# A graph network layer pair on one core: rows of x and of the result laid out by four successive nodes per partition

## The chip, the core and the metric

The kernel runs on one core of a Trainium2 chip. The metric is the device time of one execution in microseconds (us), 556.91 us as the median of three runs (556.08 to 558.59). Engines are named as in the profile: PE is TensorE's matmul, PEld its weight load, DVE VectorE, ACT ScalarE, POOL GpSimd; SPq and ACTq are the queues on which SyncE and ScalarE issue their transfers.

## The reference

There are N = 12500 nodes with rows of 128 numbers, and 200000 edges sorted by their destination `dst`, each with a row of 64 and one of 128 numbers. All is fp32. Two layers are applied, each as x + layer(relu(layernorm(x))):

```python
# layer 0, with h = relu(layernorm(x))
aggregated = segment_sum(edge_attr_64 @ W_edge.T, dst) / clip(degree, 1)
x = x + concat([h @ W_self.T, aggregated @ W_neigh.T], 1) @ W_final.T + b_final
# layer 1, with h = relu(layernorm(x))
agg = segment_sum(edge_attr_128, dst)
x = x + relu(concat([h, agg], 1) @ W1 + b1) @ W2 + b2
```

## The kernel before

**The sums of edges.** The edges are cut into 128 chunks of some 1600, taken one in each step t of the program. SyncE loads a chunk's two kinds of rows into one of five slots (`ring128`, `ring64`, L394), and waits for PE to be done with the chunk five steps earlier before it does. DVE builds one-hot matrices (L1013), PE multiplies edge rows by them (L631, L633 for the 128 features, L649 for the 64, L654 and L658 for the counts), and DVE adds the result to `agg` at a place read at run time (L1043). `agg` lies with features on partitions and nodes along the free dimension: 3 planes, the first with the 128 summed features, the other two with the 64 and the degree.

**The nodes.** They are taken in 25 groups: group 0 has 256 nodes, groups 1 to 23 have 512, group 24 the last 468. A group has 2 or 4 tiles of 128 nodes (`tiles_of`), and x lies in `x0[partition, tile, feature]`: node j*128 + p of a group is row p of tile j. `SEQ` is the order in which groups are finished, group 24 first and group 0 last. A table made before the program is built (`SELF`, `TAKE`) gives the step at which each group's work is put among the chunks: x is loaded six steps ahead of its use (`load_x`, L828 to L831), ACT normalizes it, PE transposes tile by tile (`turn`, L669) and multiplies by the weights (`own_part`, L678). Once all of a group's sums are complete, `neigh` (L694) takes 128 columns of `agg` as the stationary operand for each tile and each of planes 1 and 2, so that the product comes out with nodes on partitions. `hidden` multiplies with the weights `w1b` stationary and the group's 512 columns of plane 0 as the moving operand (L706), then with `w1a` and the transposed h (L708). `output` (L715) brings nodes back on partitions, DVE adds (L1157), and ACT issues the store (`store`, L839 to L842).

Of an fp32 product PE's records show two, each with a weight load and a matmul; a transpose has one. So the 98 tiles give 424 records on L694 (some groups have their sums in two places, which are then both multiplied), and 54 on L706.

**The tables.** In the first 46 us PE also transposes the table of destinations, `table` (L583). Its stationary operand is 32 partitions by 128 columns, read in steps of `R` elements: `.rearrange("c (p r) -> c r p", r=R)`. R is 13 for the first of its four calls, and 3, 6 and 4 for the three that follow.

Of the kernel before, what the change touches and what calls it, by code (L numbers as in the profile page):

```python
# [14 lines left out]
P = 128  # L15
# [12 lines left out]
GN = 4  # L28
# [7 lines left out]
X_SEMS = 8  # L36
# [39 lines left out]
def build_gnn(nc, x, dst, edge_attr_128, edge_attr_64, W_self, W_neigh, W_edge, W_final, b_final,  # L76
# [5 lines left out]
    NT = -(-N // P)  # L82
    LAST_N = N - (NT - 1) * P
# [19 lines left out]
    NG = 1 + -(-(N - FIRST_W) // GW)  # L103

    def begin_of(g):
        return FIRST_W + (g - 1) * GW if g else 0

    def end_of(g):
        return min(N, begin_of(g + 1))

    def tiles_of(g):
        return -(-(end_of(g) - begin_of(g)) // P)
# [87 lines left out]
    for q in range(NG - 1, -1, -1):  # L200
# [2 lines left out]
            t -= 1  # L203
        SELF.insert(0, t)
    assert SELF[0] >= 0, SELF
    TICKS = CH + 13

    def x_done(q):

        return sum(32 if SEQ[k] == NG - 1 else 16 for k in range(q % X_SEMS, q + 1, X_SEMS))  # L210


    HOT_SUMS, ADDED, LOADED, in_slot = [0], [0], [], [0] * SLOTS
# [37 lines left out]
    with ExitStack() as ctx:  # L251
# [128 lines left out]
        @block.sync  # L380
        def _(sp):
            sp.wait_ge(s_dst_clear, 1)
            z0 = 32 * UNITS * P
            sp.dma_start(dst_i[0:32, :], dst[0:z0].rearrange("(r e) -> r e", r=32)).then_inc(s_dst0, 16)

            def load_edges(t):
                c = ORDER[t]
                slot, e0, R = t % SLOTS, first_edge(c), run_of(c)
                if t >= SLOTS:
                    sp.wait_ge(s_mm, t - SLOTS + 1)  # L390
                nb = 2 if c == CH - 1 else PARTS[c // 32]
                e1 = e0 + nb * R * P
                for ring, feats in ((ring128, edge_attr_128), (ring64, edge_attr_64)):
                    sp.dma_start(ring[:, slot, 0:nb * R, :].rearrange("p (b r) f -> p b (r f)", b=nb),  # L394
                                 feats[e0:e1, :].rearrange("(b p r) f -> p b (r f)", p=P, r=R)).then_inc(s_load[slot], 16)
                    if c == CH - 1:
                        sp.dma_start(ring[0:H, slot, 6, :], feats[e1:E, :]).then_inc(s_load[slot], 16)

            load_edges(0)
            for r0, r1, e0, w in ((96, 126, first_edge(96), 12 * P), (126, 127, first_edge(126), 12 * P),  # L400
                                  (127, 128, first_edge(127), LAST_E), (32, 96, z0, 12 * P)):
                sp.dma_start(dst_i[r0:r1, 0:w], dst[e0:e0 + (r1 - r0) * w].rearrange("(r e) -> r e", e=w)).then_inc(s_dst, 16)
            rest = 12 * P - LAST_E
            sp.dma_start(dst_i[127:128, LAST_E:12 * P], dst[E - rest:E].rearrange("(r e) -> r e", r=1)).then_inc(s_dst, 16)
            for t in range(1, CH):
                load_edges(t)
            sp.wait_ge(s_store, 16 * (NG + 1))

            def general():
                sp.dma_start(gen_dst_i, dst.rearrange("(p e) -> p e", p=GP)).then_inc(s_gdst, 16)  # L410

                def group(g):
                    with sp.Fori(0, PASSES) as w:
                        with sp.Fori(0, GC) as c:
                            sp.wait_ge(s_gmm, (g * PASSES + w) * GC + c + 1)
                            for ring, feats in ((gen_r128, edge_attr_128), (gen_r64, edge_attr_64)):
                                sp.dma_start(ring, feats.rearrange("(p c r) f -> p c (r f)", p=GP, r=GR)[
                                    :, bass.ds(c, 1), :].rearrange("p o f -> p (o f)")).then_inc(s_gload, 16)
                    sp.wait_ge(s_gst, g * 32 + 32)
                    if not isinstance(g, int):  # L420
                        rows = x[bass.ds(g * GW, GW), :].rearrange("(j p) f -> p j f", p=P)
                        sp.dma_start(x0[:, 0:2, :], rows[:, 0:2, :]).then_inc(s_gx, 16)
                        sp.dma_start(x0[:, 2:4, :], rows[:, 2:4, :]).then_inc(s_gx, 16)
                        sp.wait_ge(s_gstep, g * GSTEPS + GSTEPS + 1)
                        rows = out[bass.ds(g * GW, GW), :].rearrange("(j p) f -> p j f", p=P)
                        sp.dma_start(rows[:, 0:2, :], x0[:, 0:2, :]).then_inc(s_gst, 16)
                        sp.dma_start(rows[:, 2:4, :], x0[:, 2:4, :]).then_inc(s_gst, 16)
                    else:
                        n0 = g * GW
                        sp.dma_start(x0[:, 0, :], x[n0:n0 + P, :]).then_inc(s_gx, 16)  # L430
                        sp.dma_start(x0[0:LAST_N, 1, :], x[n0 + P:N, :]).then_inc(s_gx, 16)
                        sp.wait_ge(s_gstep, g * GSTEPS + GSTEPS + 1)
                        sp.dma_start(out[n0:n0 + P, :], x0[:, 0, :]).then_inc(s_gst, 16)
                        sp.dma_start(out[n0 + P:N, :], x0[0:LAST_N, 1, :]).then_inc(s_gst, 16)
                        sp.wait_ge(s_gst, g * 32 + 64)

                every_group(sp, group)

            otherwise(sp, general)
# [3 lines left out]
        def _(pool):  # L443
# [19 lines left out]
            const(nc.gpsimd.memset(w_c[H:H + 1, 1, D:D + 1], 1.0))  # L463
            assert own_const[0] == N_CONST

            nc.gpsimd.memset(x0[:, NT - 1, :], 0.0).then_inc(s_xpad, 1)

            def steps_of(k):

# [102 lines left out]
        def _(pe):  # L572
# [108 lines left out]
            def neigh(q):  # L681
                g = SEQ[q]
                pe.wait_ge(s_added, ADDED[min(CH, TAKE[q])])
                for i, (k, _) in enumerate(FOLDS):
                    if k == q:
                        pe.wait_ge(s_fold, 2 * i + 2)
                if q:
                    pe.wait_ge(s_x1, q)
                else:
                    pe.wait_ge(s_untab, 4)  # L690
                parts = [(a, k) for a in columns_of(g) for k in range(2)]
                for j in range(tiles_of(g)):
                    for i, (a, k) in enumerate(parts):
                        last = nc.tensor.matmul(ps_nb[:, j // 2, j % 2, :], agg[:, 1 + k, a + j * P:a + (j + 1) * P], w_c[:, k, :],  # L694
                                                start=i == 0, stop=i == len(parts) - 1)
                last.then_inc(s_nb, 1)

            def hidden(q):
                g = SEQ[q]
                w = tiles_of(g) * P  # L700
                if q:
                    pe.wait_ge(s_hr, q)
                else:
                    pe.wait_ge(s_gen, 1)
                for i, a in enumerate(columns_of(g)):
                    nc.tensor.matmul(ps_hid[:, 0:w], w1b[:], agg[:, 0, a:a + w], start=i == 0, stop=False)  # L706
                pe.wait_ge(s_tpc, tp_use["n", q] + 1)
                nc.tensor.matmul(ps_hid[:, 0:w], w1a[:], h2T[:, 0:w], start=False, stop=True).then_inc(s_hid, 1)  # L708

# [100 lines left out]
        def _(act):  # L810
# [6 lines left out]
            def load_x(q):  # L817
                g = SEQ[q]
                n0, n1, j0 = begin_of(g), end_of(g), tile_of(g)
                if q >= X_SEMS:  # L820
                    act.wait_ge(s_x[q % X_SEMS], x_done(q - X_SEMS))
                if SCRATCH[0] <= g <= SCRATCH[1]:
                    act.wait_ge(s_viol, 1)
                    act.wait_ge(s_wsb, 3)
                if g == NG - 1:
                    act.wait_ge(s_xpad, 1)
                    m = n1 - LAST_N
                    act.dma_start(x0[:, j0:NT - 1, :], x[n0:m, :].rearrange("(j p) f -> p j f", p=P)).then_inc(s_x[q % X_SEMS], 16)  # L828
                    act.dma_start(x0[0:LAST_N, NT - 1, :], x[m:n1, :]).then_inc(s_x[q % X_SEMS], 16)
                else:  # L830
                    act.dma_start(x0[:, j0:j0 + tiles_of(g), :], x[n0:n1, :].rearrange("(j p) f -> p j f", p=P)).then_inc(s_x[q % X_SEMS], 16)  # L831

            def store(q):
                g = SEQ[q]
                n0, n1, j0 = begin_of(g), end_of(g), tile_of(g)
                act.wait_ge(s_rowc, row_use["n", q] + 1)
                if g == NG - 1:
                    m = n1 - LAST_N
                    act.dma_start(out[n0:m, :].rearrange("(j p) f -> p j f", p=P), x0[:, j0:NT - 1, :]).then_inc(s_store, 16)  # L839
                    act.dma_start(out[m:n1, :], x0[0:LAST_N, NT - 1, :]).then_inc(s_store, 16)  # L840
                else:
                    act.dma_start(out[n0:n1, :].rearrange("(j p) f -> p j f", p=P), x0[:, j0:j0 + tiles_of(g), :]).then_inc(s_store, 16)  # L842

            def inputs(t):
                for q in range(NG):
# [480 lines left out]
```

## Time and profile before

| | |
|---|---|
| median of three runs | 556.91 us |
| the profiled execution's own time | 556.97 us |
| its span, first to last instruction | 555.1 us |
| PE busy, share of the span | 503.9 us, 91% |
| DVE / POOL / ACT busy | 390.6 / 368.4 / 151.5 us |
| granted TensorE clock, mean | 0.966 |
| bytes moved | 169.53 MB, mean 305 GB/s |

"Busy" is the time in which at least one of an engine's instructions runs. PE records overlap (a 64-column matmul is shown as 228 ns long, yet a new one starts every 28 ns on average), so the cost of a matmul in a stream is read from the chain of work, where each piece is the time until the next one begins. Idle time of PE put down to "issue" is time in which it waited for nothing that the profile shows. The DMA share is the mean busy share of the core's 16 DMA engines.

### The profile page before, as it was taken

How to read it: one execution, taken by the hardware profiler on the slowest of the kernel's cores; microseconds unless marked ns; L12 is line 12 of the kernel's file. 1: busy time of each engine (PE TensorE's matmuls, PEld its weight loads, DVE VectorE, ACT ScalarE, POOL GpSimd, SP SyncE). 2: the span in 40 equal slices, each digit the busy share in tenths (PEclk: the TensorE clock that was granted, in tenths of full speed). 3: DMA queues.
4: the chain of work that ended last, by engine and by line, in shares of the span. 5: the costliest groups of instructions: out<-in, count | busy, mean ns of one | idle time of the engine just before them, and what ended most of it. 6: DMA issues, size and time to landing. Idle time of an engine off the chain costs nothing.

```text
span 555.1 us, 25952 instructions
## 1 busy us (share of the span) xinstructions
PE 503.9 (91%) x10989; PEld 450.1 (81%) x10989; DVE 390.6 (70%) x1230; ACT 151.5 (27%) x353; POOL 368.4 (66%) x524
## 2 busy tenths in 40 slices
PE   5568879899989999999999999998999999999993
PEld 4457768789878898888988898888888888988782
DVE  5434698776896768967798688789669877567322
ACT  0011101332233332342234224333323332313101
POOL 2735947667577776785768777885866765845730
PEclk9767899999999999999999999999999999999996
DMA  8924999999999998999999999999999998959910
GB/s 282 388 58 148 380 354 359 374 339 322 312 347 303 341 349 303 367 301 313 341 323 355 333 331 323 369 320 304 325 320 358 329 322 277 382 221 310 378 41 13
DMA packets 113229, 169.53 MB, mean 305 GB/s; under 512 B 5486, under 2 KB 84310, under 8 KB 113111
## 3 DMA queue, kind: packets, MB, share of 16 engines
q1 hardware_dynamic: 85843, 154.42, 79.7%
q10 hardware_dynamic: 27268, 13.43, 8.3%
q8 instruction: 88, 1.44, 1.1%
q14 instruction: 30, 0.25, 0.1%
HBM read 161.43 MB, written 6.40 MB: 302 GB/s over the span
## 4 chain that ended last, share of the span: by engine, by line
PE 81%; issue 6%; DVE 4%; DVEq 1%; ACT 0%; POOL 0%
PE ps L631 28%; PE ps L649 15%; PE ps L694 9%; PE ps L706 5%; PE ps L633 5%; PE ps L678 5%; PE ps L669 4%; PE ps L715 4%; PE ps L708 4%; DVE agg L1043 2%; PE ps L658 1%; DVE x L1157 1%; DVE onehot L1013 1%; DVE bn L1137 0%; DVEq L1043 0%
## 5 line engine op out<-in xcount | busy, mean ns | idle before, releaser
L631 PEld LDWEIGHTS ps<-onehot,ring 128*64 128x64 f32 x3126 | 198.8, 141 | 30.8 <-issue 22.6
L631 PE MATMUL ps<-onehot,ring 128*64 128x64 f32 x3126 | 217.2, 228 | 6.5 <-issue 4.6
L633 PE MATMUL ps<-onehot,ring 128*64 128x64 f32 x3126 | 217.3, 228 | 4.7 <-issue 4.7
L522 POOL TENSOR_TENSOR hot_part<-onehot 128x384 bf16<-128x384 f32 (+2 forms) x128 | 116.7, 912 | 152.3 <-DVE onehot L1013 150.6
L633 PEld LDWEIGHTS ps<-onehot,ring 128*64 128x64 f32 x3126 | 198.8, 141 | 5.4 <-issue 5.4
L1043 DVE TENSOR_TENSOR agg<-ps,agg 128x128 f32 (+1 forms) x319 | 95.0, 298 | 120.1 <-PE ps L658 95.9
L1013 DVE TENSOR_TENSOR onehot<-iota_win,rel 128x384 f32<-128x384 f32 (+3 forms) x192 | 164.5, 857 | 0.2
L649 PE MATMUL ps<-onehot,ring 128*64 128x64 f32 x3126 | 121.9, 226 | 7.2 <-issue 7.1
L649 PEld LDWEIGHTS ps<-onehot,ring 128*64 128x64 f32 x3126 | 109.2, 141 | 7.4 <-issue 7.2
L694 PEld LDWEIGHTS ps<-w_c,agg 128*128 128x128 f32 x424 | 49.8, 191 | 7.3 <-DVE agg L1043 3.7
L694 PE MATMUL ps<-w_c,agg 128*128 128x129 f32 x424 | 52.3, 276 | 3.3 <-issue 2.3
L522 POOL TENSOR_TENSOR hot_sum<-hot_part 128x128 bf16<-128x128 bf16 x96 | 44.7, 466 | 7.5
L875 ACT ACTIVATE hn<-x,nmr,rstd 128x128 f32<-128x128 f32 x98 | 40.4, 483 | 22.5 <-DVE nmr L1104 22.4
L903 ACT ACTIVATE h<-x,nmr,rstd 128x128 f32<-128x128 f32 x98 | 40.4, 484 | 15.5 <-DVE nmr L1149 15.5
L918 ACT ACTIVATE hid<-ps,b_col 128x512 f32<-128x512 f32 (+1 forms) x25 | 17.0, 679 | 93.2 <-PE ps L708 93.2
L500 POOL TENSOR_TENSOR x<-x,b_bc 128x512 f32<-128x512 f32 (+1 forms) x25 | 35.6, 1424 | 10.2 <-ACT h L903 10.2
L522 POOL TENSOR_TENSOR hot_sum<-hot_sum,hot_part 128x128 bf16<-128x128 bf16 x64 | 34.9, 545 | 5.0
L508 POOL MEMSET agg<- 128x1536 f32 (+2 forms) x26 | 35.5, 1366 | 0.0
L487 POOL TENSOR_TENSOR x<-x,b_bc 128x512 f32<-128x512 f32 (+1 forms) x25 | 34.2, 1369 | 0.0
L883 ACT COPY hT<-ps 128x512 f32<-128x512 f32 (+1 forms) x25 | 14.5, 579 | 70.5 <-PE ps L669 70.5
L890 ACT COPY own<-ps 128x512 f32<-128x512 f32 (+1 forms) x25 | 14.5, 579 | 67.3 <-PE ps L678 64.4
L494 POOL TENSOR_TENSOR x<-x,own 128x512 f32<-128x512 f32 (+1 forms) x25 | 31.9, 1275 | 0.0
(118 smaller groups left out, 568.7 us busy)
## 6 DMA issues: line engine op xcount, KB each, us to landing
ring<-in_edge_attr_dram SPq DMA_DIRECT2D x95, 768.0 KB, 5.5
ring<-in_edge_attr_dram SPq DMA_DIRECT2D x96, 384.0 KB, 7.0
ring<-in_edge_attr_dram SPq DMA_DIRECT2D x32, 832.0 KB, 6.2
ring<-in_edge_attr_dram SPq DMA_DIRECT2D x32, 416.0 KB, 7.7
x<-in_x_dram ACTq DMA_DIRECT2D x23, 256.0 KB, 6.3
out_dram<-x ACTq DMA_DIRECT2D x23, 256.0 KB
x<-in_dst_dram SPq DMA_DIRECT2D x1, 384.0 KB
x<-in_dst_dram SPq DMA_DIRECT2D x1, 208.0 KB, 3.6
```

Of the source, the lines that this page charges most:

```text
L487: nc.gpsimd.tensor_tensor(rows, rows, b0_bc[:, :].unsqueeze(1).to_broadcast([P, nt, D]), ALU.add).then_inc(s_xb, 1)
L500: nc.gpsimd.tensor_tensor(rows, rows, b2_bc[:, :].unsqueeze(1).to_broadcast([P, nt, D]), ALU.add).then_inc(s_x1b, 1)
L508: nc.gpsimd.memset(agg[:, :, a:b], 0.0).then_inc(s_zero, 1)
L522: nc.gpsimd.tensor_tensor(out, a, b, ALU.add).then_inc(s_hotsum, 1)
L631: nc.tensor.matmul(bank[0:H, o:o + WIN], ring128[0:K, slot, u, 0:H], hots, start=u == 0, stop=r == R - 1, skip_group_check=True)
L633: nc.tensor.matmul(bank[H:P, o:o + WIN], ring128[0:K, slot, u, H:D], hots, start=u == 0, stop=r == R - 1, skip_group_check=True)
L649: nc.tensor.matmul(bank[feats, o:o + WIN], ring64[0:K, slot, u, :], onehot[0:K, hot, u, :], start=False, stop=True, skip_group_check=True)
L694: last = nc.tensor.matmul(ps_nb[:, j // 2, j % 2, :], agg[:, 1 + k, a + j * P:a + (j + 1) * P], w_c[:, k, :], start=i == 0, stop=i == len( ...
L875: last = nc.scalar.activation(hn[:, j, :], x0[:, j0 + j, :], ACT.Relu, bias=nmr1[:, u, j:j + 1], scale=rstd1[:, u, j:j + 1])
L903: last = nc.scalar.activation(h2[:, j, :], x0[:, j0 + j, :], ACT.Relu, bias=nmr2[:, u, j:j + 1], scale=rstd2[:, u, j:j + 1])
L1013: made = nc.vector.tensor_tensor(onehot[:, t % HOTS, a:b, :], iota_win[:, :].unsqueeze(1).to_broadcast([P, b - a, WIN]), rel[:, c // 32, a ...
L1043: nc.vector.tensor_tensor(here, ps[:, t % BANKS, o:o + w * WIN].rearrange("p (a n) -> p a n", a=w), here, ALU.add).then_inc(s_added, 1)
```

## The change

Row p of tile j in a group with `nt` tiles now holds node p*nt + j instead of node j*128 + p. A partition so has four successive nodes (two in group 0), which are 2048 successive bytes (1024) in x and in the result: one transfer row instead of four of 512 bytes. The last group's 468 nodes fill 117 partitions of all four of its tiles, where before they filled three tiles and 84 partitions of the fourth; so one transfer loads and one stores it instead of two, and the area cleared before its load has four tiles instead of one.

`agg` keeps its order. So PE picks every fourth column of it (every second in group 0): as stationary operand for `neigh`, 128 columns in steps of 4 elements (16 bytes), and as moving operand for `hidden`, 512 columns in the order 0, 4, 8, ..., 1, 5, ....

```diff
@@ the end of SyncE's program
-            sp.wait_ge(s_store, 16 * (NG + 1))
+            sp.wait_ge(s_store, 16 * NG)
@@ GpSimd, before its first sums
-            nc.gpsimd.memset(x0[:, NT - 1, :], 0.0).then_inc(s_xpad, 1)
+            nc.gpsimd.memset(x0[:, NT - GN:NT, :], 0.0).then_inc(s_xpad, 1)
@@ TensorE, neigh(q)
-                        last = nc.tensor.matmul(ps_nb[:, j // 2, j % 2, :], agg[:, 1 + k, a + j * P:a + (j + 1) * P], w_c[:, k, :],
+                        last = nc.tensor.matmul(ps_nb[:, j // 2, j % 2, :], agg[:, 1 + k, a + j:a + tiles_of(g) * P:tiles_of(g)], w_c[:, k, :],
                                                 start=i == 0, stop=i == len(parts) - 1)
@@ TensorE, hidden(q)
-                    nc.tensor.matmul(ps_hid[:, 0:w], w1b[:], agg[:, 0, a:a + w], start=i == 0, stop=False)
+                    sums_128 = agg[:, 0, a:a + w].rearrange("f (p j) -> f j p", j=tiles_of(g))
+                    nc.tensor.matmul(ps_hid[:, 0:w], w1b[:], sums_128, start=i == 0, stop=False)
@@ ScalarE, load_x(q)
-                    m = n1 - LAST_N
-                    act.dma_start(x0[:, j0:NT - 1, :], x[n0:m, :].rearrange("(j p) f -> p j f", p=P)).then_inc(s_x[q % X_SEMS], 16)
-                    act.dma_start(x0[0:LAST_N, NT - 1, :], x[m:n1, :]).then_inc(s_x[q % X_SEMS], 16)
-                else:
-                    act.dma_start(x0[:, j0:j0 + tiles_of(g), :], x[n0:n1, :].rearrange("(j p) f -> p j f", p=P)).then_inc(s_x[q % X_SEMS], 16)
+                nt, m = tiles_of(g), (n1 - n0) // tiles_of(g)
+                act.dma_start(x0[0:m, j0:j0 + nt, :], x[n0:n1, :].rearrange("(p j) f -> p j f", j=nt)).then_inc(s_x[q % X_SEMS], 16)
@@ ScalarE, store(q)
-                    act.dma_start(out[n0:n1, :].rearrange("(j p) f -> p j f", p=P), x0[:, j0:j0 + tiles_of(g), :]).then_inc(s_store, 16)
+                nt, m = tiles_of(g), (n1 - n0) // tiles_of(g)
+                act.dma_start(out[n0:n1, :].rearrange("(p j) f -> p j f", j=nt), x0[0:m, j0:j0 + nt, :]).then_inc(s_store, 16)
```

The order of work on PE, DVE, POOL and SyncE is the same in both. On ACT two transfers fewer are issued. This is the head of ACT's program before, where the weights' transfers and then those of group 24's x stand:

```order
L815 DMA b_bc<-in_L_gnn_b_dram 128x128
L815 DMA b_col<-in_L_gnn_b_dram 128x1
L828 DMA x<-in_x_dram 128x3x128
L829 DMA x<-in_x_dram 84x128
L856 ACT_TABLE_LOAD
L856 COPY x<-ps 128x256
```

and this is the same place now:

```order
L818 DMA b_bc<-in_L_gnn_b_dram 128x128
L818 DMA b_col<-in_L_gnn_b_dram 128x1
L831 DMA x<-in_x_dram 117x512
L852 ACT_TABLE_LOAD
L852 COPY x<-ps 128x256
```

The shape of a full group's load goes from `128x4x128` to `128x512`, a row of 512 numbers in one piece; the store's goes the same way.

## Rows read from the trace of the kernel before

**Rows 1.** The page, sections 1 and 4 (busy; the chain that ended last).
```profile
PE 503.9 (91%) x10989; PEld 450.1 (81%) x10989; DVE 390.6 (70%) x1230; ACT 151.5 (27%) x353; POOL 368.4 (66%) x524
...
PE 81%; issue 6%; DVE 4%; DVEq 1%; ACT 0%; POOL 0%
```

**Rows 2.** Three stretches: length, PE busy (records), granted clock, DMA share, GB/s.
```profile
0.00:75.00 75.00, 49.07 (x930) 0.82 0.74 260
75.00:545.00 470.00, 451.17 (x10051) 1.00 0.93 319
545.00:555.10 10.10, 3.62 (x10) 0.51 0.06 18
```

**Rows 3.** Whom PE waited for, 75 to 545 us: total us, times, longest.
```profile
PE ps L649 <- issue: 5.2, 8, 1.4
PE ps L631 <- issue: 3.9, 3, 1.7
PE ps L633 <- issue: 2.7, 4, 1.0
PE ps L694 <- issue: 2.3, 2, 1.4
PE ps L694 <- DVE agg L1043: 1.1, 3, 0.6
PE ps L678 <- DVE x L1157: 1.0, 2, 0.7
PE ps L678 <- issue: 0.7, 1, 0.7
```

**Rows 4.** Whom SyncE's queue waited for, 75 to 555 us.
```profile
SPq L394 <- PE ps L658: 334.9, 113, 6.5
SPq L367 <- DMA out_dram<-x: 29.7, 1, 29.7
```

**Rows 5.** Page, sections 3 and 6: queues' packets, MB, share; issues, median us to landing.
```profile
q1 hardware_dynamic: 85843, 154.42, 79.7%
q10 hardware_dynamic: 27268, 13.43, 8.3%
...
ring<-in_edge_attr_dram SPq DMA_DIRECT2D x96, 384.0 KB, 7.0
...
x<-in_x_dram ACTq DMA_DIRECT2D x23, 256.0 KB, 6.3
```

**Rows 6.** The chain, 300 to 318 us: start us, us until the next piece, what.
```profile
301.77 1.05 PE ps L706 x2
302.83 0.86 PE ps L708 x2
...
307.49 1.79 PE ps L694 x16
```

**Rows 7.** Groups of PE's instructions by shape: busy us, mean ns of one.
```profile
L694 PE MATMUL ps<-w_c,agg 128*128 128x129 f32 x424 | 52.3, 276 | 3.3 <-issue 2.3 <-DVE agg L1043 1.1
...
L706 PE MATMUL ps<-agg,w1b 128*128 128x512 f32 x52 | 28.3, 633 | 0.0
```

**Rows 8.** Timeline, PEld, the tables' loads in steps of 3, 6 and 4 elements.
```profile
23.53 1.45 PEld L583 LDWEIGHTS ps<-ident,x 32*128 32x128 f32 x12 [6.99 <-DVE x L993]
...
33.66 1.68 PEld L583 LDWEIGHTS ps<-ident,x 32*128 32x128 f32 x12 [4.17 <-DVE x L993]
...
44.21 1.51 PEld L583 LDWEIGHTS ps<-ident,x 32*128 32x128 f32 x12 [3.93 <-DVE x L993]
```

**Rows 9.** Lines 583 and 600, their loads: ns min/median/max; then L583's three stretches.
```profile
L583 PEld LDWEIGHTS ps<-ident,x x49: 188/208/236, 7.4 to 45.5; 32*128 32x128 f32 x49
...
L600 PEld LDWEIGHTS ps<-ident,x x2: 183/204/224, 35.4 to 35.5; 128*128 128x128 f32 x2
...
44.20:45.90 1.70, 1.64 (x12) 1.51 (x12) 0.50 0.57 229
```

**Rows 10.** Timeline, the start: POOL's clear, ACT's first loads of x, DVE's wait.
```profile
2.63 0.31 POOL L461 MEMSET w_c<- 128x258 f32 x1
...
3.29 0.21 POOL L466 MEMSET x<- 128x128 f32 x1
...
5.84 0.50 ACTq L828 DMA_DIRECT2D x<-in_x_dram  x1
...
10.91 0.99 POOL L522 TENSOR_TENSOR hot_part<-onehot 128x384 bf16<-128x384 f32 x1 [7.41 <-DVE onehot L1013]
11.93 0.16 DVE L1167 CAST firsts<-x 32x2 f32<-32x2 int32 x1 [1.11 <-DMA x<-in_dst_dram]
```

More of the change, by code:

```diff
@@ L205, in build_gnn @@
     assert SELF[0] >= 0, SELF
+    assert all((end_of(g) - begin_of(g)) % tiles_of(g) == 0 for g in range(NG))
     TICKS = CH + 13
     def x_done(q):
-        return sum(32 if SEQ[k] == NG - 1 else 16 for k in range(q % X_SEMS, q + 1, X_SEMS))
+        return sum(16 for k in range(q % X_SEMS, q + 1, X_SEMS))
     HOT_SUMS, ADDED, LOADED, in_slot = [0], [0], [], [0] * SLOTS
@@ L836, in store @@
                 act.wait_ge(s_rowc, row_use["n", q] + 1)
[L837 to L841, printed above, removed]
-                    act.dma_start(out[n0:n1, :].rearrange("(j p) f -> p j f", p=P), x0[:, j0:j0 + tiles_of(g), :]).then_inc(s_store, 16)
+                nt, m = tiles_of(g), (n1 - n0) // tiles_of(g)
+                act.dma_start(out[n0:n1, :].rearrange("(p j) f -> p j f", j=nt), x0[0:m, j0:j0 + nt, :]).then_inc(s_store, 16)
             def inputs(t):
```

## The prediction

> **What bounds the kernel now.** I read the busy times and the chain of work that ended last first. PE is busy 91% of the span, and 81% of the chain is PE's own work, with 6% "issue" and 4% DVE [rows 1]. Then the stretches: from 75 to 545 us PE is busy for 451.17 of 470 us at the full granted clock, so 18.8 us are left idle there; 75 us of start and 10 us of tail lie around it [rows 2]. Nearly all of that idle time is "issue" (5.2 + 3.9 + 2.7 + 2.3 + 0.7 = 14.8 us), none is a wait for a DMA of edges or of x [rows 3]. The reader is to see two things that look alike and are not: the DMA engines are as busy as PE (share 0.93), but it is SyncE that waits for PE, 113 times for 334.9 us together, before it may refill a slot [rows 4]. A load of edges lands some 7.0 us after its issue [rows 5], and with five slots it is issued four steps before its use; a step is 4.2 us (470 us over the 113 waits). The DMA side has some 9 us in hand at each step. PE sets the pace, so what counts is whether PE's new access patterns cost time; what the DMA saves is mostly hidden.
>
> **Term 1, the loads of L694 in steps of four.** Sixteen of its records take 1.79 us of the chain, 112 ns each [rows 6]. In that time 129 columns are streamed and the next 128 are loaded, so `agg` is read at 128/112 = 1.14 elements a ns. There are 424 records [rows 7]; the last 8 belong to group 0, with steps of two. All stand on the path, 424 x 0.112 = 47 us. What would steps of four do? No row shows this instruction with steps, but the tables' transposes load 128 fp32 columns in steps of 3, 6 and 4. Twelve such loads take 1.45, 1.68 and 1.51 us [rows 8]; take away the last one's length (some 0.21 us) and divide by eleven: 113, 134 and 118 ns from one load to the next. One load by itself is 208 ns in the median (188 to 236), and the same kind of load without steps, L600, is 183 and 224, mean 204, at a granted clock of 0.50 in both [rows 9]. So steps cost these loads nothing that can be seen, and at step four the chip reads 128/118 = 1.08 elements a ns or more. That is within 5% of what L694 needs. Bounds: 0 if the 118 ns is the transposes' own pace, and (118 - 112) x 424 = +2.5 us if it is the reading's limit; a gain is excluded, since a stepped read cannot fetch fewer bytes. I take 0, as the three step sizes show no trend (6 is slower than 4, but 3 equals the others).
>
> **Term 2, the moving columns of L706 in steps of four.** L708, which streams 512 contiguous columns twice, takes 0.86 us of the chain, 430 ns a record or 1.19 elements a ns; L706 takes 1.05 us, the same and a weight load that nothing hides [rows 6]. There are 52 such records on 512 columns [rows 7] and two of 256 in the tail. No row shows a moving fp32 operand with steps. The nearest is again the stepped load, 1.08 elements a ns at least. Bounds: 0 above, and 430 x (1.19/1.08 - 1) = 44 ns a record, x 54 = +2.4 us, below; again no gain. I take 0, because the rate that the stream needs is the rate at which the loads were seen to run, at one access per 16 bytes, with no sign of a limit.
>
> The Trainium skill speaks against this change: "SBUF — State Buffer", at its note on SBUF cachelines, says that SBUF reads in lines of 16 bytes, that full bandwidth wants two or more hits in a line, and that an access which crosses to a new line pays a penalty. A step of four fp32 elements meets every line once. By that rule terms 1 and 2 would not be 0; the page gives no price. Steps of 4 and of 6 elements in the tables' loads do the same, and [rows 9] show no penalty there, so by the trace the rule does not bind at this rate. What it would do if it did is the first rival.
>
> **Term 3, the transfers.** The queue of x and the result (ACT's, with the weights) takes 27268 packets for 13.43 MB and 8.3% of the engines' time; SyncE's takes 79.7% for 154.42 MB [rows 5]. Per packet that is 27 ns for 492 bytes against 82 ns for 1799, so 18.2 against 21.8 bytes a ns. With rows of 2048 bytes, ACT's queue at SyncE's rate would take 13.43/154.42 x 79.7 = 6.9%: 1.4 points less. A small packet is thus only a sixth dearer per byte. On the path this is worth nothing by itself: PE waits for no edges, x lands in 6.3 us with six steps, 25 us, of lead, and the slots' 9 us in hand is the cover. If that cover were gone, the price of 1.4 points would be 7.8 us of the span. One thing may profit: the "issue" waits. If they are fetches of PE's instructions that queue among data on the same engines (I have no row that proves it), they would shrink with the queueing. Bounds: 0, and, for a queue whose delay goes as load/(1 - load), 0.93 to 0.916 is 13.3 to 10.9, -18% of 14.8 us = -2.7 us. It could also be that larger packets hold a fetch up longer; the packets of 2048 bytes are no larger than the mean of those already there, so I bound that at +0.3 us. I take -0.4.
>
> **Term 4, the start and the end.** POOL's clear grows from 128 to 512 columns: 0.21 us now; from 128x258 at 0.31 us I get some 0.5. It ends near 3.9 us, ahead of ACT's load of x at 5.84, and POOL then waits for DVE until 10.91 [rows 10]: hidden. Without that cover it would be 0.3 us. ACT issues one transfer less there (0.5 us); next on ACT is a copy that waits long for PE. Group 24's x now goes in larger packets beside the first edges and destinations, for whose last part DVE waits 1.11 us at 11.93; its 234 KB are there either way, so -0.1 to +0.3 us, taken as 0. At the end, group 0's 128 KB are 128 packets instead of 256 after the last DVE instruction; at 27 ns and 16 engines the whole is 0.43 us now, so at most -0.1 us. I take 0 for both together.
>
> **Sum.** 0 + 0 - 0.4 + 0 on the profiled execution's own 556.97 us (span 555.1 and 1.9 around it) is 556.6 us. That execution stands 0.06 us above the median of the three runs, so no correction: 556.6 us.
>
> **Rivals.**
>
> *Steps halve the reading rate of the moving operand (slower).* Place: L706, each group's hidden layer. Then each record of 512 columns takes another 430 ns, on PE, with nothing to hide it: 52 x 0.43 = +22.4 us, 579 us. If the stationary reads halved as well, a load of 128 would need some 0.11 us more, 416 x 0.107 = +44.5 us on top, 623 us. It decides from the point where a stepped read falls under 1.14 elements a ns. For it: moving and stationary operands need not be fetched alike, and only loads with steps were seen, on 32 partitions and at half the clock. Against it: those loads, at the same absolute rate. This is the cacheline rule of the Trainium skill turned into a mechanism.
>
> *Steps cost a tenth (slower).* The upper bounds of terms 1, 2 and 4 come true: +2.5 + 2.4 + 0.3 = +5.2, 562 us. For it: 118 against 112 ns. Against it: a transpose has a tail of its own in those 118 ns.
>
> *The instruction waits shrink (faster).* Term 3 at its low end with a shorter end: 554.1 us, and less if I mistake how they depend on the load; 553 at the least. For it: they are 14.8 us of PE's idle time, and DMA is 93% busy in the same stretch. Against it: only 1.4 points of load go.
>
> *The transfers stay in rows of 512 bytes.* Then term 3 is 0 and the time 557.0. The shapes of the changed kernel's transfers, 128x512, speak against it; it makes no difference to the chances.
>
> **How the numbers follow.** No change: 0.67. The instruction waits shrink by enough: 0.13. A tenth: 0.08. Halved, in one of its forms: 0.12. A measurement of this kernel can tell about 0.5% (2.8 us) from no change; its own three runs span 0.45%. The range goes from 553.0 (the low ends of terms 3 and 4 and the scatter of the median, 1 us) to 562.8 (the tenth's 562 with 0.6 of scatter); outside are the halved case and some 0.03 below. Faster by over 0.5%: 0.13 and a little of the likeliest case, 0.14. Slower: 0.08 + 0.12, 0.20 less 0.01 where the tenth stays under the bound, 0.19. Same: 0.67.
>
> **What would show it.** Right: sixteen records of L694 still take 1.79 us of the chain and two of L706 1.05 us; ACT's queue falls from 27268 packets to some 8500 (25000 rows of 512 bytes become 6282 packets) and to about 7%; SyncE still waits for PE over 110 times; PE's "issue" waits stay between 12 and 17 us. Wrong: L706 at 1.9 us for its two records or L694 over 1.9 us for sixteen; a wait of PE for edges after 75 us; the "issue" total under 10 us with the span shorter by as much, which would say that I priced the DMA's load too low.

## The result, and the profile after

The changed kernel takes 619.42 us (median of four runs, 617.27 to 620.37) against 557.75 us for the kernel before on the same chip: ratio 1.111, 95% interval 1.106 to 1.116. The forecast of 556.6 us was wrong, and so was its range. The time is near the 623 us of the first rival, halved reading of both operands, to which the forecast gave 0.12 in all its forms.

Sections 1, 3 and 4 of the page (busy; the queue of x and the result with packets, MB and share; the chain) now read:

```profile
PE 571.9 (93%) x10989; PEld 497.5 (81%) x10989; DVE 387.5 (63%) x1230; ACT 151.3 (25%) x353; POOL 366.9 (59%) x524
...
q10 hardware_dynamic: 8612, 13.43, 6.1%
...
PE 85%; DVE 4%; issue 3%; DVEq 1%; ACT 0%
```

PE has 68 us more to do with the same 10989 records [rows 1]. The queue of x and the result fell from 27268 packets to 8612, as the prediction said [rows 5]. The chain, 306 to 313 us and at the end (start us, us until the next piece, what; lines 696, 709 and 711 are 694, 706 and 708 of before), says where the 68 us are:

```profile
306.59 1.98 PE ps L709 x2
308.56 0.86 PE ps L711 x2
309.42 3.61 PE ps L696 x16
...
603.76 1.22 PE ps L696 x8
...
609.19 0.85 PE ps L709 x2
```

Sixteen records of `neigh` take 3.61 us instead of 1.79, and two of `hidden` 1.98 instead of 1.05; L711, contiguous, is as before at 0.86 [rows 6]. Group 0, last, reads in steps of two: its eight records take 1.22 us (1.17 before), its two of `hidden` 0.85 as before (these at a granted clock of 0.50 in both kernels, so they say nothing of the full clock). The groups by shape (busy us, mean ns of one) say the same:

```profile
L696 PE MATMUL ps<-w_c,agg 128*128 128x129 f32 x424 | 102.1, 396 | 3.3 <-DVE agg L1039 1.7 <-issue 1.4
L709 PE MATMUL ps<-agg,w1b 128*128 128x512 f32 x52 | 52.3, 1103 | 0.0
```

Then the stretches (length, PE busy with its records, clock, DMA share, GB/s), the middle one from the same work of the start to group 0's `neigh`. First the kernel after, then that before cut at the same work:

```profile
0.00:73.10 73.10, 45.97 (x936) 0.86 0.76 269
73.10:603.70 530.60, 521.10 (x10037) 0.99 0.81 282
603.70:616.70 13.00, 4.83 (x18) 0.66 0.04 14
```

```profile
75.00:541.90 466.90, 450.01 (x10043) 1.00 0.94 321
```

The bill: 26 x (3.61 - 1.79) = 47.3 us for `neigh` and 26 x (1.98 - 1.05) = 24.2 us for `hidden`, 71.5 us together; PE's busy time in the middle stretch grew by 71.1. Its idle time there shrank from 16.9 to 9.5 us, 7.4 us given back, and the stretch grew by 63.7. Start and tail are 1.9 and 0.2 us shorter: 61.6 us, the difference of the spans (616.7 - 555.1). The two stepped reads so account for PE's added work to within 0.4 us. PE's "issue" waits there are 7.7 us together, 14.8 before [rows 3]. SyncE still waits for PE 112 times, 393.6 us now against 334.9 [rows 4]: the transfers have more in hand than before, not less.

### The profile page after: what moved, and what is told of

Same layout as the page of the kernel before. It is cut to its first block, busy times and chain, and to the rows that moved or that the text cites. A ratio compares the mean times of both kernels' runs of the same rounds, so it can differ in the third digit from the quotient of the medians.

```text
span 616.7 us, 25950 instructions
## 1 busy us (share of the span) xinstructions
PE 571.9 (93%) x10989; PEld 497.5 (81%) x10989; DVE 387.5 (63%) x1230; ACT 151.3 (25%) x353; POOL 366.9 (59%) x524
## 3 DMA queue, kind: packets, MB, share of 16 engines
q10 hardware_dynamic: 8612, 13.43, 6.1%
## 4 chain that ended last, share of the span: by engine, by line
PE 85%; DVE 4%; issue 3%; DVEq 1%; ACT 0%
PE ps L633 25%; PE ps L696 16%; PE ps L651 14%; PE ps L709 8%; PE ps L718 4%; PE ps L671 4%; PE ps L680 4%; PE ps L635 4%; PE ps L711 3%; DVE agg L1039 1%; PE ps L660 1%; DVE onehot L1009 0%; DVEq L1017 0%; DVE x L989 0%; DVEq L1039 0%
## 5 line engine op out<-in xcount | busy, mean ns | idle before, releaser
L633 PEld LDWEIGHTS ps<-onehot,ring 128*64 128x64 f32 x3126 | 197.7, 141 | 33.4 <-issue 27.3
L633 PE MATMUL ps<-onehot,ring 128*64 128x64 f32 x3126 | 215.6, 227 | 8.9 <-issue 7.0
L635 PE MATMUL ps<-onehot,ring 128*64 128x64 f32 x3126 | 215.7, 227 | 1.8 <-issue 1.8
L635 PEld LDWEIGHTS ps<-onehot,ring 128*64 128x64 f32 x3126 | 197.7, 141 | 1.9 <-issue 1.9
L1009 DVE TENSOR_TENSOR onehot<-iota_win,rel 128x384 f32<-128x384 f32 (+3 forms) x192 | 157.5, 821 | 0.2
L651 PE MATMUL ps<-onehot,ring 128*64 128x64 f32 x3126 | 118.2, 223 | 2.9 <-issue 2.9
L651 PEld LDWEIGHTS ps<-onehot,ring 128*64 128x64 f32 x3126 | 106.2, 139 | 3.0 <-issue 2.7
L696 PEld LDWEIGHTS ps<-w_c,agg 128*128 128x128 f32 x424 | 100.5, 326 | 6.5 <-DVE agg L1039 4.4
L696 PE MATMUL ps<-w_c,agg 128*128 128x129 f32 x424 | 102.1, 396 | 3.3 <-DVE agg L1039 1.7
L709 PE MATMUL ps<-agg,w1b 128*128 128x512 f32 (+1 forms) x54 | 53.4, 1085 | 0.0
L1116 DVE TENSOR_SCALAR deg<-ps 128x4 f32<-128x4 f32 (+1 forms) x25 | 4.0, 161 | 70.2 <-PE ps L696 70.2
L502 POOL TENSOR_TENSOR x<-x,b_bc 128x512 f32<-128x512 f32 (+1 forms) x25 | 35.7, 1427 | 10.3 <-ACT h L899 10.3
L711 PEld LDWEIGHTS ps<-h2T,w1a 128*128 128x128 f32 x50 | 10.5, 213 | 33.1 <-issue 32.8
```

Source lines behind the costliest of these rows:

```text
L502: nc.gpsimd.tensor_tensor(rows, rows, b2_bc[:, :].unsqueeze(1).to_broadcast([P, nt, D]), ALU.add).then_inc(s_x1b, 1)
L633: nc.tensor.matmul(bank[0:H, o:o + WIN], ring128[0:K, slot, u, 0:H], hots, start=u == 0, stop=r == R - 1, skip_group_check=True)
L635: nc.tensor.matmul(bank[H:P, o:o + WIN], ring128[0:K, slot, u, H:D], hots, start=u == 0, stop=r == R - 1, skip_group_check=True)
L651: nc.tensor.matmul(bank[feats, o:o + WIN], ring64[0:K, slot, u, :], onehot[0:K, hot, u, :], start=False, stop=True, skip_group_check=True)
L709: nc.tensor.matmul(ps_hid[:, 0:w], w1b[:], sums_128, start=i == 0, stop=False)
L1009: made = nc.vector.tensor_tensor(onehot[:, t % HOTS, a:b, :], iota_win[:, :].unsqueeze(1).to_broadcast([P, b - a, WIN]), rel[:, c // 32, a ...
```

## The experiments

**One part at a time.** The first three kernels split the change. The kernel before, run beside them, took 557.35 us (median of 23 runs); gains and losses in us are the ratio's, on that time. The diffs of this section show only the operands that change. `e1_loads` is the kernel before with this:

```diff
-agg[:, 1 + k, a + j * P:a + (j + 1) * P]
+agg[:, 1 + k, a + j:a + tiles_of(g) * P:tiles_of(g)]
```

> The kernel before, with one part of the change: neigh takes its stationary columns of agg in steps of four; x and the result keep their old rows, so each node's neighbour part is that of another node. Theory A (a step of 16 bytes halves the rate at which a product's fp32 operand is read, stationary and moving alike): sixteen records of L694 go from 1.79 to 3.61 us of the chain, 416 x 0.114 = +47 us, less some 7 us of instruction waits that get shorter: 598 us (592 to 605), ratio 1.07. Rival B (the loads are free, as the tables' stepped loads were, and the changed kernel's time came from elsewhere, such as the new rows of x): 557 us. Rival C (the slowing needs the new transfers as well): 557 to 570 us.

Measured: 599.31 us, ratio 1.0767 (1.071 to 1.082), +42.7 us. `e2_moving` is the kernel before with the other read:

```diff
-nc.tensor.matmul(ps_hid[:, 0:w], w1b[:], agg[:, 0, a:a + w], start=i == 0, stop=False)
+sums_128 = agg[:, 0, a:a + w].rearrange("f (p j) -> f j p", j=tiles_of(g))
+nc.tensor.matmul(ps_hid[:, 0:w], w1b[:], sums_128, start=i == 0, stop=False)
```

> The kernel before, with one part of the change: hidden streams its moving columns of agg in the order 0, 4, 8, ..., 1, 5, ...; the rest is as before, so each node's summed edges are those of another node. Theory A: two records of L706 go from 1.05 to 1.98 us of the chain, 26 x 0.93 = +24 us, less a few us of shorter instruction waits: 578 us (572 to 582), ratio 1.04. Rival B (moving operands are free): 557 us.

Measured: 576.02 us, ratio 1.0334 (1.028 to 1.039), +18.6 us. In each chain only the stepped line is slower; that of `e1_loads`, then that of `e2_moving`:

```profile
299.52 1.06 PE ps L706 x2
300.58 0.86 PE ps L708 x2
301.44 3.61 PE ps L694 x16
```

```profile
290.80 1.97 PE ps L707 x2
292.77 0.86 PE ps L709 x2
293.63 1.78 PE ps L694 x16
```

Each read costs by itself what it costs in the changed kernel, without the new transfers. `e3_rows` is the changed kernel with both edits undone, so it has the transfers alone.

> The changed kernel's transfers (rows of 2048 bytes, the last group in one transfer) with the old contiguous reads of agg by TensorE, so sums and nodes don't match. It prices the gain that the change was to bring. Theory A (PE sets the pace, edges have 9 us in hand): within 1.5 us of 557. Rival (PE's instruction waits are fetches that queue among data on the DMA engines): down to 554. Rival (larger packets hold the fetches up): up to 560.

Measured: 555.14 us, ratio 0.9956 (0.992 to 0.9992), -2.5 us (0.4 to 4.5): a gain that is barely told from none. Its q10 has 6.6% of the engines' time:

```profile
q10 hardware_dynamic: 8612, 13.43, 6.6%
```

The three add up to 42.7 + 18.6 - 2.5 = 58.8 us, against 61.9 measured for the whole (0.111 x 557.75); the intervals of the four cover the difference.

**What a step costs, alone.** `m1_full` and `m2_half` have streams of like instructions on an idle chip, such as

```python
for _ in range(12):
    last = nc.tensor.matmul(ps[:, 0, 0:128], wide[0:128, 0:512:4], wide[0:128, 0:128], start=True, stop=True)
```

> Nothing of the layers is computed; the result is zeros. TensorE alone runs streams of like instructions at the full clock on an idle chip (no other engine, no transfers): fp32 products with the 128 stationary columns in steps of 1, 2, 3, 4, 6, 8, 13; with 512 moving columns in steps of 1, 2, 3, 4, 6, 8; with 32 rows; transposes of 128 and of 32 rows; bf16 loads and moving columns. Theory A1 (a read needs two hits in a 16-byte line): steps 1 and 2 alike, some 110 ns a record, from step 4 on twice as long whatever the step, step 3 in between; transposes too, if they are at the full clock. Theory A2 (only products of fp32 in two records suffer): transposes at all steps alike at 110 to 120 ns. Theory A3 (128 rows at once are needed for it): 32 rows alike at all steps. Rival (contention with DVE, POOL or transfers on the same memory made it): no step costs anything here.

> The same streams, shorter, each after a pause of TensorE long enough that the granted clock is half; the result is zeros. Theory A4 (the limit is one of the memory in absolute time, about 1.77 ns for each new line): at half clock contiguous products take 213 ns a record and steps of four next to nothing more; transposes, which read 128 columns in 107 ns at half clock, would take 226. Theory A5 (the limit is in TensorE's own clocks): a step of four doubles the record here too, to some 430 ns. The tables' transposes in the kernel (118 ns at step four and half clock) should be met again by the streams of 32 rows.

The timeline of PE in `m1_full` (start us, us, line, shape, records); lines 51, 54, 57, 60, 69 are products with their 128 loaded columns in steps of 1, 2, 3, 4 and 13, lines 81, 84, 87, 93 have 512 moving columns in steps of 2, 3, 4 and 8, lines 105 and 108 are transposes of 128 rows with loads in steps of 4 and 13, lines 111, 114 and 120 transposes of 32 rows with loads in steps of 1, 2 and 4:

```profile
31.17 2.84 PE L51 MATMUL ps<-wide 128*128 128x128 f32 x24
33.84 2.99 PE L54 MATMUL ps<-wide 128*128 128x128 f32 x24
36.67 4.33 PE L57 MATMUL ps<-wide 128*128 128x128 f32 x24
40.84 5.76 PE L60 MATMUL ps<-wide 128*128 128x128 f32 x24
...
57.52 6.32 PE L69 MATMUL ps<-wide 128*128 128x128 f32 x24
...
79.07 4.66 PE L81 MATMUL ps<-wide 128*128 128x512 f32 x10
83.57 6.92 PE L84 MATMUL ps<-wide 128*128 128x512 f32 x10
90.32 9.17 PE L87 MATMUL ps<-wide 128*128 128x512 f32 x10
...
108.25 9.36 PE L93 MATMUL ps<-wide 128*128 128x512 f32 x10
...
122.95 2.08 PE L105 MATMUL ps<-ident,wide 128*128 128x128 f32 x16
124.87 2.00 PE L108 MATMUL ps<-ident,wide 128*128 128x128 f32 x16
126.80 1.67 PE L111 MATMUL ps<-ident,wide 32*128 32x32 f32 x24
128.31 3.04 PE L114 MATMUL ps<-ident,wide 32*128 32x32 f32 x24
...
133.91 3.06 PE L120 MATMUL ps<-ident,wide 32*128 32x32 f32 x24
```

With the last one's length taken off, the pace of a product's load is 112, 118, 174, 233 and 257 ns. Moving columns go at 450, 675, 899 and 918 ns a record. So a step of two is nearly free, three costs half as much again, four doubles it, and from there on it hardly grows. Neither transfers nor other engines are needed for it. The transposes are another matter. With 128 rows a step of four takes (124.87 - 122.95)/16 = 120 ns at the full clock, where a product takes 233. With 32 rows it is 63 ns with contiguous columns, and 120 ns with a step of two, both at the full clock, as the granted clock in the stretches shows (the number behind the count of records); by line 120 TensorE had fallen to half, and a step of four took the same 120 ns:

```profile
126.80:128.30 1.50, 1.50 (x25) 1.00 0.00 0
128.30:131.00 2.70, 2.70 (x26) 1.00 0.00 0
...
133.90:136.70 2.80, 2.80 (x26) 0.50 0.03 6
```

A load in steps of four goes at about 0.9 ns a column in a transpose and at 1.8 ns in a product. With a step of two the two operations are alike, 120 and 118 ns.

At half clock, the loads of eight product records in steps of 1 and of 4, and of twelve transposes of 32 rows in steps of 1 and of 4 (timeline of PEld in `m2_half`); then, from PE's timeline, eight product records on 32 rows in steps of 1 and of 4:

```profile
29.82 1.78 PEld L194 LDWEIGHTS ps<-wide 128*128 128x128 f32 x8 [29.82 <-issue]
...
62.16 1.94 PEld L206 LDWEIGHTS ps<-wide 128*128 128x128 f32 x8 [9.02 <-POOLq L50]
...
246.14 1.35 PEld L274 LDWEIGHTS ps<-ident,wide 32*128 32x128 f32 x12 [9.23 <-POOLq L118]
278.55 1.51 PEld L286 LDWEIGHTS ps<-ident,wide 32*128 32x128 f32 x12 [9.37 <-POOLq L130]
```

```profile
105.37 2.07 PE L222 MATMUL ps<-wide 32*128 32x128 f32 x8 [8.38 <-POOLq L66]
116.17 2.23 PE L226 MATMUL ps<-wide 32*128 32x128 f32 x8 [8.73 <-POOLq L70]
```

This run's profile prints a clock of 1.00 throughout, but the contiguous stream goes at (1.78 - 0.33)/7 = 207 ns, about half the pace of line 51: TensorE was at its lower level. (In `m1_full`, contiguous moving columns go at 855/512 = 1.67 ns each in line 78, 73.4 to 77.2 us, where the granted clock is 0.52; 207/128 is 1.62.) There, a step of four costs a product 230 ns and a transpose 118 (the 1.51 us of [rows 8] to the digit). The 230 is what a step of four costs at the full clock too. So the limit is a time, not a count of TensorE's clocks, and A4 is right for products; it is wrong for transposes, which it put at 226. On 32 rows a step of four adds 0.16 us to eight product records, as on 128 (1.94 - 1.78), so the number of rows plays no part and A3 is wrong, as far as the half clock shows: in `m1_full` too the stepped stream on 32 rows (line 75, 235 ns) ran at a granted clock of 0.52, and no run has one at the full clock.

**Lines or steps.** `m3_pairs` has only moving patterns that tell the two apart, as

```python
wide[:, 0:2048].rearrange("k (c r) -> k c r", r=8)[:, :, 3:5]
```

> Nothing of the layers is computed; the result is zeros. TensorE alone at the full clock, fp32 products of 512 moving columns: contiguous; pairs of neighbours inside one 16-byte line with steps of 8 between pairs (0 1, 8 9, and 1 2, 9 10); pairs that straddle two lines (3 4, 11 12); fours in one line; steps of 4; the changed kernel's order (0 4 8 ..., then 1 5 9 ...); one column 512 times. Theory of lines (what costs is each change of 16-byte line, some 1.75 ns, against 0.83 ns that a column takes in the array): contiguous and fours 430 ns a record, pairs inside a line 450, straddling pairs and steps of four 900, one column 430. Rival theory of steps (each column whose address isn't the next costs extra): both kinds of pairs alike, between 450 and 900, and one column 512 times slow. bf16, one record, steps of 2, 4 and 8 elements: by lines 220, 450 and 900 ns.

Its timeline: line 51 is contiguous, 54 has pairs 0 1, 57 pairs 1 2, 60 the straddling pairs 3 4, 63 fours, 66 steps of four, 87 the changed kernel's order, 90 one column 512 times.

```profile
32.56 4.46 PE L51 MATMUL ps<-wide 128*128 128x512 f32 x10
36.85 4.75 PE L54 MATMUL ps<-wide 128*128 128x512 f32 x10
41.44 4.75 PE L57 MATMUL ps<-wide 128*128 128x512 f32 x10
46.02 9.16 PE L60 MATMUL ps<-wide 128*128 128x512 f32 x10
55.00 4.47 PE L63 MATMUL ps<-wide 128*128 128x512 f32 x10
59.31 9.16 PE L66 MATMUL ps<-wide 128*128 128x512 f32 x10
...
92.28 9.35 PE L87 MATMUL ps<-wide 128*128 128x512 f32 x10
101.45 4.49 PE L90 MATMUL ps<-wide 128*128 128x512 f32 x10
```

Per record: 430, 459, 459, 898, 431, 898, about 900 and 433 ns. Pairs cost about the same as steps of two while both lie in one 16-byte line and double when they straddle two. The theory of steps is wrong, that of lines holds: in a product, each change of line costs 898/512 = 1.75 ns, against 430/512 = 0.84 ns that a column takes in the array at the full clock. Lines of 8 bytes would have split the pairs 1 2, and lines of 32 would have held 3 4 together. This run tells the theories apart for moving columns only; for loads the steps of two and three fit lines (118 ns for 64 changes of line, 174 for 96, so 1.84 and 1.81 ns each).

**Two kernels that keep part of the change.** Both compute the whole layer pair. `e4_pairs` has two successive nodes per partition in each pair of tiles (`hidden`'s moving columns and the stores, not shown, follow the same order):

```diff
-agg[:, 1 + k, a + j * P:a + (j + 1) * P]
+agg[:, 1 + k, a + j // 2 * 2 * P + j % 2:a + (j // 2 + 1) * 2 * P:2]
-x[n0:n1, :].rearrange("(j p) f -> p j f", p=P)
+x[n0:n1, :].rearrange("(b p j) f -> p b (j f)", p=P, j=2)
```

> The whole layer pair with two successive nodes per partition instead of four: rows of 1024 bytes in x and the result, agg read in steps of two fp32 elements (8 bytes), two reads in each 16 bytes. Theory A with a limit at one read per 16-byte line (group 0, in steps of two, cost the changed kernel 1.22 us for eight loads against 1.17): PE as before, 557 us within 1.5, and less by what the rows bring. Rival (any step costs in proportion, or the two-level order of columns does): 590 us or more.

Measured: 558.22 us, ratio 1.0035 (1.0002 to 1.0069).

```profile
300.81 1.10 PE ps L707 x2
...
306.56 1.89 PE ps L694 x16
```

Steps of two are not quite free: 26 x 0.10 + 26 x 0.05 = +3.9 us on PE, and +2.0 measured (0.1 to 3.8). That leaves some 2 us for the rows of 1024 bytes, in line with `e3_rows`, but no more than the scatter of the runs. `e5_act` has rows of 2048 bytes and gives the reordering to ScalarE. This is one of its three places, against the changed kernel; the copy of the transposed h and the reading of `hidden`'s result are reordered too:

```diff
+nc.scalar.copy(apart_t[:, i, :, 0:w].rearrange("f k (j p) -> f k j p", p=P),
+               agg[:, 1:3, at:at + w].rearrange("f k (p j) -> f k j p", j=nt))   # at the head of step TAKE[q]
-agg[:, 1 + k, a + j:a + tiles_of(g) * P:tiles_of(g)]
+apart_t[:, columns_of(g).index(a), k, j * P:(j + 1) * P]
```

> The whole layer pair with four nodes per partition and rows of 2048 bytes, TensorE reading contiguous columns only: ScalarE (27% busy) copies planes 1 and 2 of a group's sums into tile order ahead of neigh, writes the transposed h in node order, and reads the hidden layer's result from PSUM in steps of four; hidden reads agg contiguously in node order. Theory A (TensorE's stepped reads were the whole loss; rows alone are worth -2.4 us): 555 us (553 to 557) if the copies, some 1.2 us for each of 41 places, are done before neigh is reached in its step. Rival (the copy comes late, or ScalarE's stepped access is slow as well, so that neigh waits 1 us or more in each of 25 groups): 565 to 590 us.

Measured: 591.66 us, ratio 1.0552 (1.049 to 1.061); there are 27 copies, not the 41 that the expectation counted. PE's lines are near their old times (`neigh`'s records 299 ns in the mean, 276 before and 396 in the changed kernel), and it waits instead. First `neigh`'s group; then whom PE waited for (total us, times, longest); then whom ACT waited for:

```profile
L699 PE MATMUL ps<-w_c,apart_t 128*128 128x129 f32 x424 | 59.1, 299 | 20.2 <-ACT apart_t L921 20.2
```

```profile
PE ps L699 <- ACT apart_t L921: 20.2, 15, 3.0
...
PE ps L720 <- ACT own L888: 4.1, 2, 2.6
...
PE ps L673 <- ACT hT L881: 3.1, 1, 3.1
```

```profile
ACT apart_t L921 <- DVE agg L1059: 100.5, 20, 9.9
```

A copy takes 2.0 us, and it stands at the head of ACT's step, where it waits for DVE's last addition with all of ACT's other work behind it. The rival was right in both its forms. The copy comes late, and ScalarE's stepped access is slow as well: its copy of the transposed h, now written in steps of four, takes 1.11 us instead of 0.58. PE's three waits are 27 us, and `neigh`'s records are busy for 6.8 us more than before (59.1 against 52.3 [rows 7]); the loss is 31 us. The profiled execution was 4 us above the median, and how the loss splits was not pursued. With some 2.5 us to win, neither kernel that computes the whole layer pair beat the kernel before.

## Why the prediction was wrong

**What bounds the kernel** was right: PE set the pace before and after, and of the 71.1 us that PE gained in work in the middle stretch all but 7.4 lengthened it. The cover on the DMA side stood.

**Term 1** is the step that failed. It priced `neigh`'s stepped loads by the tables' stepped loads, "at the same absolute rate", and took 0 with a bound of +2.5 us; it cost 47.3 us. The rate of [rows 8, 9] was real, and `m2_half` meets it again, but it belongs to transposes. A stepped read in a product is limited at 1.75 to 1.8 ns a line, in a transpose at 0.9 ns a column. The bound was one of another operation, put forward as if it were one of the memory. The rows were misread too: 113, 118 and 134 ns for steps of 3, 4 and 6 rise with the step, where the prediction saw no trend. `m2_half` shows no rise over more steps (118, 111, 118, 136 and 112 ns for 2, 3, 4, 6 and 13), so this misreading is not what made the term fail. The comparison also hid the sign of a limit: at half clock L583 and the contiguous L600 look alike because a contiguous load takes TensorE 103 ns there anyway (line 274 of `m2_half`, (1.35 - 0.22)/11), against 118 at a step of four; `m1_full` shows 63 against 120 ns at the full clock.

**Term 2** failed in the same way: 0 taken, +2.4 us as the bound, 24.2 us measured, where the moving operand meets the same limit per line. The prediction noted that "moving and stationary operands need not be fetched alike"; in a product they meet the same limit at a step of four (899/512 = 1.76 and 233/128 = 1.82 ns a column). What wasn't alike was product and transpose.

**The rule that was set aside** was right for products. The Trainium skill's "SBUF — State Buffer", note on SBUF cachelines, wants two or more hits in a 16-byte line; the trace agrees, with 459 ns for pairs in a line and 898 for pairs across two. Where the note names four fp32 elements as the stride that is free, the measurement differs and decides: four has the full price, 233 against 112 ns, and two is the last step that is nearly free. The prediction does not mention that figure, which would have favoured the change. For transposes the rule does not describe what was measured: two hits in each line, and still 120 ns against 63.

**Term 3**: -0.4 us taken, within -2.7 and +0.3; the transfers alone gave -2.5 us (0.4 to 4.5). Sign and bounds held, though the interval goes beyond them, and the value was too small. Two slips in its working change nothing: a small packet costs a fifth more per byte (21.8/18.2), not a sixth, and the shapes give 2 x (23 x 128 + 117 + 128) = 6378 packets for x and the result, not the 6282 of the last paragraph, so 8646 in all, near the 8612 measured. PE's idle time in the middle stretch fell with the DMA share: 16.9 us at 0.94 before, and in the changed kernel 9.5 at 0.81. That fits waits for instructions queued among data, which no run here isolated. The "issue" waits of 7.7 us lie under the 10 us that the prediction named in a sign of being wrong; the other half of that sign, a span shorter by as much, can't be told apart here, as the span grew.

**Term 4** was right: start and tail moved by -1.9 and -0.2 us. The first is more than the 0.1 us foreseen. PE was busy for 3.1 us less there (45.97 against 49.07), at a granted clock of 0.86 instead of 0.82, and no run ties that to the change; it is below what the runs can tell.

**The rivals.** The halved case was worked out to +66.9 us for both operands and the measured terms are +71.5; what it left out is the 7.4 us given back by shorter idle times. It had the mechanism, the place and the price, and was given 0.12 on the strength of one analogy.

## What to carry to other kernels

Price a new access pattern from rows of the same operation at the same clock; a row of a cousin (transpose for product, half clock for full) bounds nothing until something shows that the two share their limit. When a change trades transfer layout against TensorE's read pattern, see first which of the two sets the pace: here 1.7 points of DMA time were bought with a doubled read on the engine that was 91% busy. In fp32 products at the full clock keep at least two neighbours of each 16-byte line next to each other in the order of columns.

## What the hardware showed that was not expected

- In a product at the full clock, stationary and moving fp32 operands meet the same limit, 1.75 to 1.8 ns for each change of 16-byte line at a step of four (2.0 ns for loads at a step of 13). At half clock a load in steps of four costs about the same 230 ns as at the full one, on 32 rows as on 128.
- A transpose's contiguous load of 128 fp32 columns takes 63 ns, and a step of two 120 ns (both at the full clock), so the line rule doesn't describe it: a step of two, with two columns in each line, is as slow as four. Why is open.
- Repeating a column costs nothing (433 ns a record), but reading each line four times with other lines between costs in full (about 900 ns).
- The limit is not one of every load. In `m1_full`, 32 loads of 128 bf16 columns in steps of 16, each column in a line of its own, start within 149.9 to 151.8 us at a granted clock of 1.00: 61 ns a load, 0.5 ns a column. For loads, the 1.75 to 1.8 ns are shown for fp32 products alone.

```profile
L141 PEld LDWEIGHTS ps<-narrow x32: 172/173/174, 149.9 to 151.8; 128*128 128x128 bf16 x32
```
